# Third slot's gate and up block ahead of the carry, an earlier state decay, and two changes of order and of banks in the first slot

## The reference

```python
x = x + layernorm(attention(layernorm(x)))     # lightning attention, 16 heads of 32
x = x + layernorm(ffn(layernorm(x)))           # 512 -> 1536 -> 512, weights rounded to fp8
# attention, per head and chunk of 128 tokens, S is the running state:
inter  = (q * decay_q) @ S                     # called the carry in the kernel
scores = (q @ k.T) * dmask
out    = inter + scores @ v
S      = lam_c * S + (k * decay_k).T @ v
# ffn:
down( silu(x @ gate * gate_scale) * (x @ up * up_scale) ) * down_scale
```

## Time and profile before

| | |
|---|---|
| median of 3 runs | 978.01 us (976.84 to 980.41) |
| profiled execution | 977.56 us |
| its span, first to last instruction | 975.8 us |
| mean granted TensorE clock | 0.997 of full |
| busy: TensorE / VectorE / GpSimd / ScalarE | 951.2 / 695.0 / 687.8 / 509.4 us |

### The profile page before, as it was taken

The page is one execution under the profiler, slowest core; times in us unless marked ns, Lnnn a source line. Parts: engine busy times, 40 slices in busy tenths (PEclk is TensorE's granted clock), DMA queues, the critical chain, the costliest instruction groups (busy, mean ns, idle before and its releaser), DMA issues.

```text
span 975.8 us, 21934 instructions
## 1 busy us (share of the span) xinstructions
PE 951.2 (97%) x8436; PEld 704.4 (72%) x8436; DVE 695.0 (71%) x1362; ACT 509.4 (52%) x986; POOL 687.8 (70%) x837
## 2 busy tenths in 40 slices
PE   8999999999998999999999999999999999999997
PEld 6677877777666686767677776767767786776765
DVE  6899899996888775767667576767667676766423
ACT  5656565565555554636354463636446463644522
POOL 3689988988686675849577585947658594865733
PEclk9999999999999999999999999999999999999999
DMA  9999999689976772847557384756758375522110
GB/s 284 263 304 280 308 298 285 214 228 300 240 210 139 152 195 46 199 97 159 125 135 171 69 195 90 164 120 137 158 93 195 76 174 112 139 66 44 32 36 23
DMA packets 199497, 159.87 MB, mean 164 GB/s; under 512 B 141664, under 2 KB 142048, under 8 KB 199264
## 3 DMA queue, kind: packets, MB, share of 16 engines
q1 hardware_dynamic: 198384, 157.73, 65.2%
q10 hardware_dynamic: 1008, 0.74, 0.5%
HBM read 82.93 MB, written 41.94 MB: 128 GB/s over the span
## 4 chain that ended last, share of the span: by engine, by line
PE 46%; DVE 20%; POOL 13%; issue 11%; DMA 4%; SPq 3%; ACT 2%; DVEq 0%; POOLq 0%; ACTq 0%
PE bank L932 19%; PE bank L950 16%; PE att L909 5%; DVE stats L1418 3%; POOL att_pool L1142 3%; POOL rstd L1077 2%; DVE row_max L1384 2%; DMA dram_qk<-qk_hl 2%; DVE w_pool L1555 2%; DVE state_hl L1492 2%; POOL xr L1152 1%; PE att L895 1%; DVE qk_hl L1448 1%; SPq L304 1%; DVE state L1481 1%
## 5 line engine op out<-in xcount | busy, mean ns | idle before, releaser
L932 PE MATMUL bank<-f_pool,up_q 128*128 128x256 f16 x1536 | 183.6, 273 | 4.0 <-DVE w_pool L1555 2.8
L932 PE MATMUL bank<-f_pool,gate_q 128*128 128x256 f16 x1536 | 183.5, 273 | 3.3 <-ACT w_pool L626 3.1
L932 PEld LDWEIGHTS bank<-f_pool,up_q 128*128 128x128 f16 x1536 | 148.1, 98 | 26.5 <-DVE w_pool L1555 8.4
L932 PEld LDWEIGHTS bank<-f_pool,gate_q 128*128 128x128 f16 x1536 | 146.4, 98 | 25.7 <-ACT w_pool L626 5.4
L950 PE MATMUL bank<-down_q,w_pool 128*128 128x512 f16 x744 | 163.1, 379 | 0.0
L1142 POOL TENSOR_TENSOR att_pool<-p,att_pool 128x512 f16<-128x512 f32 x128 | 145.6, 1159 | 23.7 <-ACT att_pool L578 23.7
L1555 DVE SCALAR_TENSOR_TENSOR w_pool<-bank,us_t,w_pool 128x256 f32<-128x256 f32 x192 | 84.1, 480 | 108.7 <-ACT w_pool L626 51.5
L1074 POOL TENSOR_TENSOR rstd<-mv,eps_t 128x1 f32<-128x1 f32 (+1 forms) x112 | 30.6, 273 | 180.9 <-DVE mv L1424 180.8
L950 PEld LDWEIGHTS bank<-down_q,w_pool 128*128 128x128 f16 x744 | 71.6, 98 | 84.2
L1160 POOL TENSOR_TENSOR w_pool<-w_pool 128x512 f16<-128x512 f32 x96 | 111.2, 1164 | 28.4 <-ACT w_pool L632 28.3
L578 ACT CAST att_pool<-p 128x512 f16<-128x512 f32 x128 | 75.5, 619 | 52.9 <-DVE p L1462 52.3
(11 more groups left out here) (156 smaller groups left out, 1825.4 us busy)
## 6 DMA issues: line engine op xcount, KB each, us to landing
dram_qk<-qk_hl SPq DMA_DIRECT2D x64, 256.0 KB, 3.9
att_pool<-dram_qk SPq DMA_DIRECT2D x64, 256.0 KB, 6.0
f_pool<-dram_qk SPq DMA_DIRECT2D x64, 256.0 KB, 6.2
xr<-in_x SPq DMA_DIRECT2D x31, 512.0 KB, 4.8
dram_kd<-kd_hl SPq DMA_DIRECT2D x32, 256.0 KB, 2.9
dram_v<-vv SPq DMA_DIRECT2D x32, 256.0 KB, 4.8
qn_pool<-dram_qk SPq DMA_DIRECT2D x32, 256.0 KB, 9.0
out_x<-w_pool SPq DMA_DIRECT2D x31, 256.0 KB, 2.2
```

The source lines that it names most:

```text
L932: ins = nc.tensor.matmul(b[:, j * TOK:(j + 1) * TOK], w[:, k, o * P:(o + 1) * P], x1_hl[:, v % 2, part, k], start=(k == 0 and part == 0), ...
```

## The change

Five edits in one diff:

- TensorE, slot 2 (the third slot): `gate_up(0, 0)` goes in front of `carry_and_state(2, 0)`. All other slots keep their order.
- GpSimd: `state_decay(s + 1, 0)` for slots 3 to 15 goes from the head of its slot to the end of the slot before, ahead of the root and of `final(v, 0)`. Slot 2 keeps its own at the head.
- VectorE, first slot: `state_lo(0, 0)` goes behind `k_lo(14, 2)` and masked(0, 1, 0).
- v of unit 13 goes into `b_gate` and `b_up` and not into `b_s`.
- With it the waits change: scores(0, 0, 0) ask for the v sums up to unit 12, `project_v(13, t)` for `norms_d` and `wout_scale_d` (which read those banks before), `project_qk(14, i)` for the v sum of unit 13, tile i.

```diff
         def v_bank(n, t):
-            return b_s[t][:, :] if n < LEAD else (b_gate, b_up)[t][:, :]
+            return b_s[t][:, :] if n < LEAD - 1 else (b_gate, b_up)[t][:, :]
...
                 elif i >= 2:
                     pe.wait_ge(q_d, 2 * n + i - 1)
-                elif n == LEAD:
-                    pe.wait_ge(norms_d, 2)
-                    pe.wait_ge(wout_scale_d, 1)
                 else:
                     pe.wait_ge(v_d, 2 * (n - 1) + i + 1)
...
-                if n < LEAD:
+                if n < LEAD - 1:
                     at_least(pe, v_d, 2 * (n - 1) + t + 1)
+                elif n == LEAD - 1:
+                    pe.wait_ge(*((wout_scale_d, 1) if t else (norms_d, 2)))
                 else:
                     pe.wait_ge(k_lo_d, 2 * n + t + 1)
...
                     if s == 0:
-                        pe.wait_ge(v_d, 2 * LEAD)
+                        pe.wait_ge(v_d, 2 * (LEAD - 1))
...
                 if attends:
                     scores(s, 0, 0)
+                    if s > 2:
+                        carry_and_state(s, 0)
+                gate_up(v, 0)
+                if s == 2:
                     carry_and_state(s, 0)
-                gate_up(v, 0)
...
-                if attends:
+                if s == 2:
                     state_decay(s, 0)
...
                 h_lo(v, 5)
+                if s + 1 < units:
+                    state_decay(s + 1, 0)
                 inverse_std_of(LN_Y2, v, 0)
                 final(v, 0)
...
                 masked(0, 0, 1)
-                state_lo(0, 0)
                 k_lo(LEAD, 2)
                 masked(0, 1, 0)
+                state_lo(0, 0)
                 out_sum(0, 0)
```

## The result

The changed kernel takes 970.37 us (median of 6, 968.92 to 972.28) against 977.56 for the kernel before in the same comparison (median of 6, 976.84 to 980.41). The ratio is 0.9917 with a 95% interval of 0.9898 to 0.9936: faster by 0.8%, 7.2 us in the medians where the forecast had 8.5, and 0.9 us above the forecast of 969.5. The profiled execution took 971.96 with a span of 970.1.

The account below looks back on a forecast made before the run. The prediction took TensorE as the bound, 951.2 us of a 975.8 us span, so only its waits could be won. Its terms, -5.6 - 2.3 - 0.6 = -8.5 us, gave 969.5, range 966.5 to 973.5.

Parts of the forecast that it names:

- 5.6 + 2.3: Slots 3 to 15: 5.6 us from thirteen TensorE stalls at the slots' start, 2.3 from later stalls around gate block 5.
- The chain that I named: Behind the later stalls: masked(s,0,1), probs_hi, silu 1, product 1, y moments, both roots, residuals, x1 moments, then the silu.
- C: Rival: stall returns at gate block 5, a full slot having 0.26 us to spare; 2.6 and 0.6 won, 975; chance 0.08.
- D: Rival: slower, each slot's split held by GpSimd until 438.9, some 0.65 us longer 13 times; +8.4 - 0.6, 986; chance 0.05.
- A: Rival: only stalls at the slots' start won, GpSimd's roots and residuals set the later ones; -6.2, 971.8; chance 0.14.
- 0.6 us left: First slot, masked scores ahead of the state's split: 0.6 of 3.65 us won, bounds +0.5 and -2.0.
- 1.65 us: First slot: time lost by twelve TensorE matmuls at half clock, 4.25 us in place of 2.6.
- Rival B: The first slot's moved split runs free and the slot keeps 2.0 us: -9.9, 968.1; chance 0.11.
- The landing does not move: First slot, v's banks: the q spill lands as before, so the 0.88 us wait moves; taken at 0, bounds 0 and -0.9.
- The wait only moved: Third slot, gate/up block before the carry: the 1.68 us stall moves, gate block 1 stays; 0, bounds +0.3 and -0.5.
- Rival E: TensorE's clock falls in the third slot, gate block 1 loses 1.7 us, all but some 0.2 hidden; counted inside the forecast's 0.62.
- E's full case: The clock falls in the first slot as well as the third: -7.2, 970.8.

Follow-up runs that it names:

- product_first: The kernel before with VectorE's product in front of carry and state in every slot, the decay left at the slot's head: 987.17 us, ratio 1.0082.
- split_back: The changed kernel with the state's split ahead of k_lo again in the first slot: 967.66 us, ratio 0.9894.
- decay_only: The kernel before with only the state decay moved ahead of the root in slots 3 to 15: 968.70 us, ratio 0.9904.
- decay_banks: The kernel before with the decay ahead of the root and v of unit 13 in the two other banks: 969.86 us, ratio 0.9921.
- PSUM variants: Four kernels, from the changed kernel or the one before, whose first state's split reads its source from PSUM and not SBUF: 966.27 to 967.09 us.
- no_decay: The changed kernel with the state decay back at the head of its slot: 979.53 us, ratio 1.0014.
- best_mix: The kernel before with the decay ahead of the root, first split reading PSUM, third slot's gate and up block ahead of the carry: 966.36 us, ratio 0.9891.
- banks_back: The changed kernel with v of unit 13 and its waits back in `b_s`: 969.36 us, ratio 0.9904.

## Why the prediction was right, and where it was not

**The decay: right in its way, low in size.** All thirteen stalls at the slots' start went, and the later ones too. The forecast had 5.6 + 2.3; measured are 9.07. Slots are now 42.04 or 42.71 us, and the 0.67 between them is one group of carry or state matmuls; of the waits about 0.15 us is left, at gate block 5 of slot 3, which has 42.20. Of the 1.2 us that I missed, 0.7 are nine waits of 0.07 to 0.09, eight of them at gate block 5 (slot 5: 455.90, where 455.81 was possible), which I had left out of the list: slots of 43.12 lost 0.41, where I had counted 0.30 or 0.31. The rest I can't name wait by wait. The chain that I named was the right one. In the forecast masked(s,0,1) would begin 1.5 us earlier; it did by 1.45 (9.22 to 7.77), and `product_first`, which takes the stall away and makes the chain later, shows the chain alone: slower by 9.2 in the slots. That is also the mechanism of rivals C and D. D had 0.65 for each of 13 slots, 8.4 us, if the split ended late; the split did so in `product_first`, and the price was 9.2. In the changed kernel the split took 2.27 and ended at 438.13, 7.74 behind the slot's first masked scores against 9.18 before, so D did not come. A and C fell with the stalls of the earlier trace rows. C had also been given too much: it put 0.26 us to spare into a full slot, and slot 5 had none, for it already waited 0.09 there.

**The split in the first slot: wrong in sign.** The step was masked(0,1,0) early, the clock kept up, the split held until 255.8, 0.6 us left. The first half held: from ScalarE's cast to the v block that began at 255.15 are 8.74 us before and 6.75 after, and the granted clock there is 1.00. What failed was this:

1. The four split instructions took 4.01 and not 3.0. They began where forecast, 6.37 us behind the cast (252.8 - 246.41 = 6.39). I had the four wait for the end of a q split, the decay and two splits of scores. The q split was just over when they began, so they waited for the decay, the two splits of scores and the 1.20 of kd's split. masked(0,1,1) stands 13.31 us behind the cast, against 11.97 before; I had allowed 0.37 more and it was 1.34.
2. The next state's split took 2.13 instead of 1.19. I had it "by the next state split (268.9 before)" at its old length. GpSimd's split of q started 0.23 us behind it and held it. Before, TensorE's slow v block had made q late: that split started at 269.12, after VectorE's had ended at 268.90. Giving the clock back brought q forward into VectorE's way.
3. So the half clock was worth nothing in this slot. With it (before, split_back) the second column has 27.64, without it (decay_only, decay_banks) 27.68. I had added 1.65 us as the main source of the gain; VectorE's chain was under it. In the changed kernel TensorE was ready for the second slot's carry 23.81 us behind the cast and waited until 24.89 for the held split; before it came at 23.51.

Together the move costs 1.38 us (27.64 to 29.02). The hold of the first split is most of it but not all: with its operand from PSUM the column is 25.70 with the old order and 26.20 with the new one, so 0.50 us goes to the order without any hold there, and 0.9 to the hold, which costs 1.9 in the old place and 2.8 in the new one. Rival B, the free split, had 1.4 more than the forecast; taking the hold away from the changed kernel gave 2.8. The Trainium skill ("SBUF — State Buffer", SBUF: two separate sides) gave the rule that a VectorE instruction with two SBUF inputs must take a port pair shared with GpSimd. The trace agrees: 4.01 against 1.18 us for one operand moved to PSUM. I used the rule for one split and forgot it for the next.

**v in two other banks: taken at 0.** Scores no longer waited for the last v sum, but ScalarE's wait for a spill of v ahead of its cast is 3.03 us and not 0.75. The column from v sum to cast is 9.19 and not 8.50, 0.7 us. With 1.38 this is all of the 2.07 that the first slot lost (36.14 to 38.21). The step that failed is "The landing does not move", said of the spill of q; the wait that grew is for the spill of v of the unit before. That transfer took 7.40 to 7.66 us from its issue to its landing in the seven profiles with the old banks and 8.39 to 8.83 in the seven with the moved ones (tile 0), and ScalarE's wait was 0.01 to 1.13 against 1.97 to 3.09. So the later landing goes with the banks and is not scatter; through what it does was not shown. How much of it reaches the state's cast scatters: the medians of the column are 8.50 and 9.11, and the times of the PSUM variants show no price. The remaining 1.34 of the 3.44 us lie ahead of v_sum(13,1), 237.91 before and 239.25 after. Other kernels have that point at 236.61 to 238.67, `no_decay`, with the same code up to there, at 237.43, so this is scatter of the profiled execution and not the change.

**Gate and up block ahead of the carry: 0, for the wrong reason in part.** The wait only moved, as forecast: masked(2,0,0) to the mark is 30.54 in both. Rival E came, a fall of the clock in the third slot (0.55 in the window), and it was hidden, also as forecast; the first slot had none, so E's full case, 970.8, did not come as it was put. What I had not seen is that the old order can lose too. The last column is 56.7 for all seven kernels with the new order, three of them with a fall at 300 to 306. With the old one it is 56.7 without a fall in the third slot, 57.30 with one of 3.4 us at 298.0, and 58.26 and 58.45 with one of 6.8 us at 295.1, where carry, state and gate block stand one behind another. So the old order lost up to 1.7 us in an execution whose clock fell there. That the new order would have hidden the same fall is not shown: in its profiles none is longer than 3.4 us or earlier than 300. In the medians it does not show (970.43 and 970.37), and `best_mix` too had two executions of 969.06 and 970.69 at a mean clock of 0.994 among four of 965.56 to 966.44, so it does not protect from every fall. On what lets it fall, the Trainium skill ("TensorE: Matmul & The Clock Gate", Part 1) names idleness. Here it fell at 295.1 in `decay_banks` with TensorE busy for 1.50 of the 3.40 us before, and in the same part of the slot it stayed up in `product_first` (292.80 to 296.20) with 1.52 of 3.40 busy. The waits of 1.17 and 0.51 us ahead of the fall at 306.0 stand in `banks_back` as well, which had none. What decides was not settled.

**The sum.** -9.1 in the slots, +1.4 for the split, +0.7 for v's way, +1.3 ahead of all that: -5.7, the difference of the spans (975.8 and 970.1). Without the scatter of 1.3 it makes 977.56 - 9.07 + 1.38 + 0.69 = 970.56, and the median is 970.37. The forecast came near because 1.2 us too little in the slots stood against 2.7 us too much in the first slot (0.6 promised, 2.07 lost).

## What to carry to other kernels

A wait on another engine at the head of each slot is best priced by the chain behind it and not by the stall that it shows: the same stall taken away in two ways gave 9.1 us and lost 9.2. Before an instruction with two SBUF operands is moved on VectorE, list what GpSimd runs beside its new place and beside every later one that shifts with it; reading one operand from PSUM took the question away. A stretch at half clock costs only where TensorE sets the pace, so ask first which engine would be waited for at full speed.

## What was not expected of the hardware

Four VectorE instructions of 32 x 128 elements took 1.18 us beside a busy GpSimd with one operand in PSUM, and 3.89 to 4.28 with both in SBUF; in the second group, with one long GpSimd instruction beside them, 2.13 against 1.19. The granted clock fell for 3.4 or 6.8 us at a time, at different places in kernels that differ by one edit, and cost between nothing and 1.7 us. One spill to DRAM landed 8.39 to 8.83 us behind its issue instead of 7.40 to 7.66 when a v projection went into other PSUM banks; why stays open.
